# An attention step on one core: the first two output products moved ahead of the transposes of q and of the keys

## The reference, cut to what matters

```
q = einsum('bsd,ed->bse', x, Wq)      # 32 heads of 128
k, v = the same with Wk, Wv           # 8 heads of 128
q, k = rope(rmsnorm(q)), rope(rmsnorm(k))
k_all = concat([k_cache[block_table], k]);  v_all likewise   # 512 cached keys + 128 new ones
scores = einsum('bqhd,bkhd->bhqk', q, k_all) * SCALE          # masked beyond the cache's length
o = einsum('bhqk,bkhd->bqhd', softmax(scores), v_all)
x = x + einsum('bse,de->bsd', o, Wo)
```

## Time and profile before

| | |
|---|---|
| median of 3 runs | 1414.79 us (1413.38 to 1415.3) |
| profiled execution, its own time | 1415.05 us |
| its span | 1413.3 us |
| PE busy | 1393.9 us (99%), mean granted clock 0.998 |
| PE weight loads busy | 1207.2 us (85%) |
| DVE busy | 1098.4 us (78%) |
| ACT busy | 852.1 us (60%) |
| POOL busy | 806.6 us (57%) |
| chain that ended last | PE 79%, SP's queue 14% |

### The profile page before, as it was taken

One profiled execution on the slowest core, in us unless ns is written; L12 is line 12 of the kernel. 1 busy time (PEld: TensorE's weight loads), 2 busy tenths in 40 slices (PEclk: granted clock), 3 DMA queues, 4 the chain that ended last, 5 costly groups with the idle time before them and its releaser, 6 DMA issues.

```text
span 1413.3 us, 26959 instructions
## 1 busy us (share of the span) xinstructions
PE 1393.9 (99%) x8031; PEld 1207.2 (85%) x8031; DVE 1098.4 (78%) x2231; ACT 852.1 (60%) x2092; POOL 806.6 (57%) x802
## 2 busy tenths in 40 slices
PE   7999999999999999999999999999999999999999
PEld 5888888888888888888888888888888788888887
DVE  6888888888888888888888888888888566555543
ACT  6666666666666676666667676667667323433332
POOL 7655555555555666666666666666566331444442
PEclk9999999999999999999999999999999999999999
DMA  5533333333333232322222222232332450343341
GB/s 182 162 103 106 108 115 96 110 102 102 101 106 105 70 78 69 71 65 65 66 66 66 65 75 72 64 72 46 94 81 76 131 109 23 99 135 115 113 123 68
DMA packets 191584, 129.87 MB, mean 92 GB/s; under 512 B 118976, under 2 KB 158528, under 8 KB 189008
## 3 DMA queue, kind: packets, MB, share of 16 engines
q1 hardware_dynamic: 190592, 126.97, 32.5%
q0 software_dynamic: 416, 1.11, 0.2%
q10 hardware_dynamic: 432, 0.07, 0.0%
HBM read 125.25 MB, written 24.64 MB: 106 GB/s over the span
## 4 chain that ended last, share of the span: by engine, by line
PE 79%; SPq 14%; issue 3%; DMA 1%; DVE 1%; POOL 1%; ACT 0%; ACTq 0%; DVEq 0%; POOLq 0%
PE banks L327 19%; PE banks L328 19%; PE banks L329 19%; PE banks L1444 10%; PE banks L1418 8%; SPq L347 7%; SPq L340 3%; SPq L400 3%; PE banks L1380 2%; PE banks L1670 1%; PE banks L1684 1%; PE banks L1497 1%; PE banks L1623 1%; SPq L374 1%; DMA trig<-in_trig,trig_at 1%
## 5 line engine op out<-in xcount | busy, mean ns | idle before, releaser
L747 ACT ACTIVATE prob<-prob,nbias 128x640 f32<-128x640 f32 x256 | 210.3, 822 | 156.4 <-DVE nbias L1019 156.4
L990 DVE TENSOR_TENSOR pt_pair<-banks,pt_pair 128x640 fp32r<-128x640 f32 x256 | 211.0, 824 | 108.1 <-ACT pt_pair L743 105.8
L1019 DVE CUSTOM_DVE_ANT_0 prob<-banks,mask,q_rs 128x640 f32<-128x640 f32 x256 | 220.2, 879 | 37.1 <-PE banks L329 37.1
L1444 PE MATMUL banks<-w_pair,o_pair 128*128 128x512 f32 x768 | 224.4, 414 | 0.0
L743 ACT ACTIVATE pt_pair<-banks 128x640 fp32r<-128x640 f32 x256 | 179.1, 700 | 46.6 <-PE banks L1418 46.5
L1418 PE MATMUL banks<-ident,prob 128*128 128x128 f32 x1280 | 184.9, 275 | 4.3 <-DVE pt_pair L990 4.2
L1418 PEld LDWEIGHTS banks<-ident,prob 128*128 128x128 f32 x1280 | 146.6, 140 | 47.5 <-issue 36.2
L327 PE MATMUL banks<-w_pair,x_pair 128*128 128x256 f32 (+1 forms) x512 | 178.4, 348 | 0.8 <-DVE acc L1044 0.8
L328 PE MATMUL banks<-w_pair,x_pair 128*128 128x256 f32 (+1 forms) x512 | 173.2, 338 | 0.0
L329 PE MATMUL banks<-w_pair,x_pair 128*128 128x256 f32 (+1 forms) x512 | 172.7, 337 | 0.0
L327 PE MATMUL banks<-kt_pair,qt_pair 128*128 128x320 f32 x512 | 164.1, 321 | 0.9 <-DVE kt_pair L990 0.9
(11 more groups left out here) (194 smaller groups left out, 3446.3 us busy)
## 6 DMA issues: line engine op xcount, KB each, us to landing
w_raw<-in_w_att SPq DMA_DIRECT2D x56, 320.0 KB, 3.2
w_raw<-in_fw SPq DMA_DIRECT2D x66, 256.0 KB, 3.4
x_raw<-in_xT SPq DMA_DIRECT2D x64, 256.0 KB, 3.2
kt_all<-in_kT SPq DMA_DIRECT2D x128, 128.0 KB, 2.5
kv_raw<-in_kv SPq DMA_DIRECT2D x384, 32.0 KB, 1.6
kt_raw<-kt_all SPq DMA_DIRECT2D x38, 256.0 KB, 3.0
kv_raw<-in_kv SPq DMA_DIRECT2D x608, 16.0 KB, 1.5
fb_all<-in_gu_b SPq DMA_DIRECT2D x32, 176.0 KB
```

The source lines that it names most:

```text
L747: act.activation(prob[:, h, :], prob[:, h, :], ACT.Exp, bias=nbias[:, h:h + 1], scale=-1.0, accum_out=psum_row[:, h:h + 1]).then_inc(exped, 1)
L990: dve.tensor_tensor(pair[1], src, pair[0].bitcast(F32), ALU.subtract).then_inc(lo_sem, 1)
L1019: dve.tensor_tensor_reduce(out=prob[:, h, :].rearrange("p (a n) -> p a n", a=2), in0=score_ps[h % 2][:, :, 0:HALF], in1=mask[:, n % B, :]. ...
L1444: last = pe.matmul(misc_ps, o_pair[:, j, h, :], w_pair[:, k, ds(at + h * HID, HID)], start=i == 0, stop=i == 3 * REP - 1)
```

## The change

In PE's list of a step the two matmuls `project_out(n - 1, 0, 2)` go from behind the transposes of q and of the keys to a place ahead of them, directly behind `scores(n, 3)`. `transpose_p(n, 1)` then follows directly on the key transposes.

```
                 transpose_p(n, 0)
                 scores(n, 3)
+                if not first:
+                    project_out(n - 1, 0, 2)
                 transpose_q(n + 1)
                 if n + 1 < BY_ROWS:
                     transpose_cached_k(n + 1, 1 - par)
                 transpose_new_k(n + 1, 1 - par)
-                if not first:
-                    project_out(n - 1, 0, 2)
                 transpose_p(n, 1)
                 if not first:
                     project_out(n - 1, 2, 10)
```

## The result

The changed kernel takes 1450.82 us (median of 6 runs, 1449.21 to 1452.5), the kernel before 1414.28 us (median of 6). The ratio is 1.0255, with a 95% interval of 1.0244 to 1.0265: 36.5 us slower. The profiled execution took 1450.55 us with a span of 1448.8 us, 35.5 us more than before. One execution of the kernel before, in the set beside the four versions from `e_p_before_keys` to `e_nine`, took 7731 us; the ratios leave it out, and it moves the median of that set by 0.13 us.

A forecast was written before the change was run, and what follows sets the result against it. It took a loop over PE, ACT and DVE through P's second and third heads as the bound. 31.5 + 9.2 + 3.0 = 43.7 us on 1415.05 gave 1458.8, stated as 1458.5 us; range 1446 to 1466.

The forecast's parts named there:

- the forecast case: Attention steps: moved matmuls wait for o, q's transposes and ACT's queue start late, P's third head too; 1458.5 us, 85%.
- The wait for o: PE, first moved output matmul: waits for DVE's low part of o, starting 0.25 us late in a late step.
- ACT's queue: ACT copies q, cached keys, new keys, then P's second head; P's copy starts 1.17 us behind the queue's start.
- the first rival: Attention steps: o's low part in time or taken earlier, q's transposes move only 0.47 us; 1436 us, 7%.
- The late steps: Steps 25 to 62, 38 in number: each 0.83 us longer, 31.5 us in all.
- The middle steps: Steps 7 to 24, with nine q and key transposes: 0.54 us each, counted 17 times, 9.2 us.
- The early steps: Steps 2 to 6, with tables on DVE: 0.59 us in each of five, 3.0 us.
- step 1's delay: Step 1: PE waits 0.75 us for the residual's first addition anyway, so a shift there costs nothing.
- First wait free: PE's wait for o's low part costs nothing, q's transposes move only 0.47 us; 1436 us, 7%.
- Faster: PE's waits before P's second and third head go: 8 us gained, 1407 us, at most 31 us, 1384 us; 3%.
- The clock: PE's new idle times drop its clock for nine matmuls in each of 61 steps: 110 us more, 1569 us; 3%.
- Absorbed: ACT and DVE make up for the delay; time stays within what can be told from no change; 2%.

The follow-up runs named there:

- e_p_before_keys: Changed kernel with ACT's copy and DVE's low part of P's second head ahead of those of the keys, PE's list untouched; 1432.67 us, ratio 1.0119.
- e_nine: Kernel before with nine instead of eight output matmuls between P's second and third head; 1411.41 us against 1414.79, ratio 0.9976.
- e_fill: Changed kernel with the last two output matmuls also moved ahead of P's third head, into the wait there; 1442.98 us, ratio 1.0196.
- e_between: Kernel before with the two output matmuls placed between q's transposes and those of the keys; 1420.11 us, ratio 1.0035.
- e_one_ahead: Changed kernel with one of the two moved output matmuls back behind the key transposes; 1438.88 us, ratio 1.0175.
- e_wait_only: Kernel before with only the wait for o's low part put ahead of q's transposes, no matmul moved; 1426.22 us against 1415.36, ratio 1.0082.
- e_swap_waits: Changed kernel with the two waits in front of P's transposes in the other order in PE's list; 1447.28 us, ratio 1.0233.

## Why the prediction was right, and which term was too large

**The mechanism.** It was the forecast case. The wait for o appears in front of the moved matmuls, ACT's queue starts late by as much as q's transposes, P's second head stands behind the keys in that queue, and P's third head on PE waits for it. The waiting time in that place is shown by the kernel that fills it (`e_fill`), the queue by the kernel that takes P out of it (`e_p_before_keys`), and the entrance to the queue by the one that lets q's transposes go first (`e_between`). The wait for o by itself is worth 10.9 us, the work moved ahead the rest: 12.7 us for the first matmul (`e_one_ahead` less `e_wait_only`), 13.0 for the second. How the rest is split between the two is less certain: the profiled spans give 13.7 and 11.8 us, and a late step grows by 0.28 and 0.22 us.

**The number.** 1450.8 us lies in the stated range of 1446 to 1466, but only in the part by which I had widened it towards the first rival; the forecast's own range began at 1453. The mechanism was right and its price in most steps 0.1 us too high.

**The late steps.** Predicted 0.83 us, measured 0.72 (17.49 for 16.77). The term that failed is the start of the first output matmul behind DVE's low part of o. I took 0.15 us, from P's transposes; it is 0.06: DVE ends at 595.77 + 0.69 = 596.46, PE starts at 596.52. The matmul of the earlier trace rows had the same 0.06 us behind its DVE instruction, and I read only the distance to its successor there. `e_swap_waits` shows what makes most of the 0.15. The other terms held: 0.33 to the second matmul and 0.23 behind it together 0.56 (597.08 - 596.52) where I had 0.58, and ACT's queue 1.17 us (597.72 to 598.89), as forecast.

**The middle steps.** Predicted 0.54 us, measured 0.44 (17.59 for 17.15), the same 0.1 us. The wait stands ahead of nine transposes here, in five rows of PE's list and not in seven. As forecast, a part of the shift is lost in slack on DVE: from q's transposes to P's third head it is 3.62 us instead of 3.90. A middle step in ACT's and DVE's rows, which answer to the earlier trace rows:

```profile
211.96 0.71 ACT L729 ACTIVATE kt_pair<-banks 128x640 fp32r<-128x640 f32 x1
...
212.70 0.82 DVE L990 TENSOR_TENSOR kt_pair<-banks,kt_pair 128x640 fp32r<-128x640 f32 x1
213.44 0.81 DVE L990 TENSOR_TENSOR pt_pair<-banks,pt_pair 128x640 fp32r<-128x640 f32 x1
```

DVE takes the keys 0.03 us behind ACT's end, so they are what it waits for. The two steps that had waited for key pages have the period of the others now, which took off 0.8 us, where I had 0.54. That the change covers this wait is likely but not shown: `e_nine`, which is faster, had none in its profile either.

**The early steps.** Predicted 0.59 us in five steps, measured 0.50 in four, steps 3 to 6 (18.19 for 17.69). Step 2 did not grow: from P's third head to P's third head it became 0.48 us shorter, and steps 0 to 2 together grew by 0.2 us, where I had 0.59. The wait of the earlier trace rows is the likely reason. The addition that PE waits for there had itself waited for a load of x; before the change:

```profile
57.15 0.69 DVE L1044 TENSOR_TENSOR acc<-banks,acc 128x512 f32<-128x512 f32 x1 [1.08 <-DMA acc<-in_x]
```

In the changed kernel's profile neither wait is there. I had let this wait absorb step 1's delay alone. The longer stretch at 1.2 GHz falls into these steps too, and its price is not told apart here.

**The sum.** By the starts of P's third head, steps 0 to 6 added 2.2 us (3.0 predicted), the middle ones 7.1 (9.2) and the late ones 27.5 (31.5), 36.7 us together (before rounding) where 43.7 were forecast. From these go 1.3 us that have nothing to do with the change: q's first transposes start at 14.42 us instead of 15.68, with the same lists up to there, and over all profiles here between 14.1 and 16.1. That leaves the 35.5 us of the spans. With 0.06 in place of 0.15 us in 60 steps the forecast would have been 5.4 us lower, 38.3 us.

**The rivals.** First wait free: no, PE waits for o in each of the 35 steps of the window (the weight loads 8.9 us in all), and 1436 us would have been 15 us too low. Faster: no; `e_between` has P's second head directly behind the key transposes and q's transposes in time, and is still 4.8 us slower. The clock: no, the granted clock is 1.00 over 630 us of late steps, with 0.41 us of PE's idle time and 25 transposes in each; the lower clock is seen only in the first steps and the last, as before the change. So neither the rule of the Trainium skill's page "TensorE: Matmul & The Clock Gate" on short repeated idle times (its section "A second HAM failure mode: psum-queue depth-cycling") nor that on transposes comes into play in these steps. I had written that PE does transposes only between its two waits; it does ten transposes and ten output matmuls there. Absorbed: no, 36.5 us are clear of the interval.

## What to carry to other kernels

Before two pieces of work change places in one engine's list, look at what the piece that comes later feeds. Here the five to nine transposes were the entrance to another engine's queue, and the last entry of that queue was what the first engine waited for next; the matmuls fed nobody soon and belonged behind. And where one chain over other engines has a fixed length (2.49 us here from one head's transposes to the next), count the work between its two ends: one matmul too few there was idle time in every step.

## What I had not expected of the hardware

The delay from the end of a DVE instruction to the PE instruction that waits for it was 0.15 us in one place and 0.06 in another, in the same kernel, 35 times each. Where two waits stand in front of an instruction, it was 0.15 with the late one written last, and 0.06 with the late one written first and the other one fulfilled long ago. Swapping them in the source moved P's transposes by that, though 0.03 us of it came back behind the first of them. Other waits of these profiles go the same way: 0.14 us for the projection in `e_fill`, whose late wait (`added`) is written last of three, and 0.06 for q's transposes in `e_wait_only`, whose late wait (`o_lo`) is written first. Only the swap changes the order and nothing else. Why it is so, no run here shows.
